# Moving the transposition of V from the DMA queue to TensorE in a layernorm, attention and linear kernel

## The reference

```python
x = x + attn(layernorm(x), Wq, bq, Wk, bk, Wv, bv)
x = x + linear(layernorm(x), weight * scale_weight[:, None], bias)
```

```python
q, k, v = (split_heads(h @ W + b) for W, b in ...)
ctx = local_attention(q, k, v)                  # window of 256 keys
idx = [0] + top_k(norm(q), 62) + [t - 1]
ctx[idx] = softmax(q[idx] @ k.T / 8) @ v
```

## Time and profile before

| | |
|---|---|
| median of 3 runs | 2140.1 us (2135.53 to 2141.93) |
| profiled execution | 2135.53 us |
| its span, first to last instruction | 2134.0 us |
| PE busy | 2102.1 us (99%) |
| PE weight loads busy | 1791.9 us (84%) |
| DVE busy | 1272.7 us (60%) |
| ACT busy | 829.0 us (39%) |
| POOL busy | 502.7 us (24%) |

### The profile page before, as it was taken

The page is one execution under the profiler, slowest core; times in us unless marked ns, Lnnn a source line. Parts: engine busy times, 40 slices in busy tenths (PEclk is TensorE's granted clock), DMA queues, the critical chain, the costliest instruction groups (busy, mean ns, idle before and its releaser), DMA issues.

```text
span 2134.0 us, 36682 instructions
## 1 busy us (share of the span) xinstructions
PE 2102.1 (99%) x12576; PEld 1791.9 (84%) x12576; DVE 1272.7 (60%) x2551; ACT 829.0 (39%) x1979; POOL 502.7 (24%) x336
## 2 busy tenths in 40 slices
PE   6999999999999999999999999999999999999999
PEld 6888888888788888887888888878888888888887
DVE  5685556545855564458555554495555566666664
ACT  4334445552354455532544545225445551000000
POOL 2231122124411321144112211432123112212121
PEclk9999999999999999999999999999999999999999
DMA  4333232223332322233323221323223113333331
GB/s 161 103 99 88 75 106 64 62 69 99 109 90 75 106 60 65 69 95 103 88 85 88 76 68 42 104 69 83 65 71 120 51 59 146 128 138 128 138 128 69
DMA packets 192506, 194.29 MB, mean 91 GB/s; under 512 B 91984, under 2 KB 157590, under 8 KB 192400
## 3 DMA queue, kind: packets, MB, share of 16 engines
q1 hardware_dynamic: 184752, 175.19, 27.7%
q10 hardware_dynamic: 4320, 15.73, 1.8%
q0 software_dynamic: 3328, 2.17, 0.5%
HBM read 122.73 MB, written 51.44 MB: 82 GB/s over the span
## 4 chain that ended last, share of the span: by engine, by line
PE 85%; DVE 11%; issue 2%; ACT 1%; DMA 1%; DVEq 0%; SPq 0%; POOL 0%; ACTq 0%; POOLq 0%
PE proj L566 40%; PE proj L742 15%; PE pv L691 10%; PE turn L679 5%; PE score L664 5%; PE pv L722 3%; DVE top_idx L1317 2%; DVE x_norm L1319 2%; PE score L704 2%; DVE top_val L1315 2%; DVE q_sq L1282 2%; PE turn L714 1%; PE turn L731 1%; PE proj L831 1%; DVE norms L1284 1%
## 5 line engine op out<-in xcount | busy, mean ns | idle before, releaser
L566 PE MATMUL proj<-xT_hi,w_lo 128*128 128x512 f32 x1536 | 408.7, 397 | 0.0
L566 PE MATMUL proj<-xT_hi,w_hi 128*128 128x512 f32 x1536 | 402.8, 404 | 2.5 <-issue 1.5
L566 PE MATMUL proj<-xT_lo,w_hi 128*128 128x512 f32 x1536 | 381.4, 390 | 0.0
L434 POOL CAST w_hi<-w_raw 128x1024 fp32r<-128x1024 f32 x96 | 100.7, 1049 | 1171.6 <-PE proj L566 901.7
L566 PEld LDWEIGHTS proj<-xT_lo,w_hi 128*128 128x128 f32 x1536 | 288.3, 188 | 62.9
L566 PEld LDWEIGHTS proj<-xT_hi,w_lo 128*128 128x128 f32 x1536 | 280.6, 188 | 62.0
L566 PEld LDWEIGHTS proj<-xT_hi,w_hi 128*128 128x128 f32 x1536 | 274.2, 188 | 63.4 <-DVE kT_lo L1300 2.7
L1002 ACT ACTIVATE probs<-score,neg_max 128x256 f32<-128x256 f32 (+1 forms) x512 | 229.3, 463 | 167.4 <-DVE neg_max L1366 120.1
L691 PEld LDWEIGHTS pv<-v_nat,pT 128*128 128x128 f32 x2048 | 248.1, 191 | 10.4
L691 PE MATMUL pv<-v_nat,pT 128*128 128x64 f32 x2048 | 242.3, 271 | 0.0
L436 POOL TENSOR_TENSOR w_lo<-w_raw,w_hi 128x1024 fp32r<-128x1024 f32 x96 | 232.3, 2420 | 7.8
(11 more groups left out here) (165 smaller groups left out, 2988.3 us busy)
## 6 DMA issues: line engine op xcount, KB each, us to landing
w_raw<-in_wstream SPq DMA_DIRECT2D x96, 512.0 KB
x_buf<-in_rows SPq DMA_DIRECT2D x55, 512.0 KB, 4.1
q_rows<-q_nat SPq DMA_DIRECT2D x64, 256.0 KB
ctx_rows<-ctx_out SPq DMA_DIRECT2D x128, 128.0 KB, 1.9
q_store<-ctx_rows SPq DMA_DIRECT2D x30, 512.0 KB
out<-q_store ACTq DMA_DIRECT2D x30, 512.0 KB, 2.6
q_store<-in_cols SPq DMA_DIRECT2D x28, 512.0 KB
q_store<-in_rows SPq DMA_DIRECT2D x8, 512.0 KB, 5.2
```

The lines of the kernel that those rows point to most:

```text
L434: pool.tensor_copy(w_hi[b][:, :], w_raw[b][:, :]).then_inc(w_hi_set, 1)
L566: mm = pe.matmul(proj[:, bank, :], w[b][:, k * P:k * P + P], x[:, k, half * HALF:half * HALF + HALF], start=(m == 0), stop=(m == 23), skip ...
```

## The change

The 16-bit halves, the transposing DMAs and the joining copies go. PE transposes `vT`, which is now packed (1024 columns), against the identity into `misc` in three groups: tiles 0, 8, 1 and 2 after the scores of step 0; tiles 3 to 6 ahead of `turn_p` of step 0; tile 7 ahead of `weigh` of step 0. ACT copies each group to `v_nat` (`v_nat_out`): ahead of the exponentials of step 0, ahead of `p_out` of step 0, and ahead of `p_out` of step 1. The edge tiles have 64 rows; the upper 64 rows of those tiles in `v_nat` are set to zero once. Since `misc` is used in turns, `m_turned` and `m_set` now count four uses a unit. `vT` and `probs` also change places as scratch memory at the start.

```diff
-        vT = sb("vT", [P, (TILES + 1) * P])
-        v_parts, v_turned = (sb(name, [P, TILES + 1, 2, P], U16) for name in ("v_parts", "v_turned"))
+        vT = sb("vT", [P, SEQ])
...
+        V_GROUPS = [[(0, 0), (8, 128), (1, 256), (2, 384)], [(3, 0), (4, 128), (5, 256), (6, 384)], [(7, 0)]]
+        V_PIECES = [[(64, 0, TILES, 2, 0), (P, 1, 1, 2, 256)], [(P, 3, 1, 4, 0)], [(P, 7, 1, 1, 0)]]
...
-            def turn_v(n, hp, h):
-                sp.wait_ge(v_parted, n * (2 * PAIRS) + 2 * hp + h + 2)
-                apart(sp)
-                sp.dma_start_transpose(v_turned[:, V_TILES[h], :, :].rearrange("p t s r -> p (t s) r"),
-                                       v_parts[:, V_TILES[h], :, :].rearrange("p t s c -> p (t s c)")).then_inc(v_moved[h], 16)
...
             def weigh(u, s):
                 pe.wait_ge(pv_free, u * EVENTS + s + 1)
-                if s < 2:
-                    pe.wait_ge(v_set, 2 * u + s + 1)
...
+            def turn_v(u, g, first):
+                if g == 0:
+                    pe.wait_ge(proj_free[0], first + 3)
+                else:
+                    pe.wait_ge(m_set, u * MISC + g)
+                apart(pe)
+                for j, col in V_GROUPS[g]:
+                    a, z = tile_tokens(j)
+                    mm = pe.transpose(misc[0:z - a, col:col + P], vT[:, a:z], ident[:, :])
+                mm.then_inc(m_turned, 1)
...
             def turn_gq(u):
+                pe.wait_ge(m_set, u * MISC + 3)
                 pe.wait_ge(pad_set, u + 1)
...
                 scores(u, 0, first)
+                turn_v(u, 0, first)
                 part(0)
                 if ahead:
                     turn_ahead(1)
+                turn_v(u, 1, first)
                 if ahead:
                     part(1)
...
                 if not ahead:
                     part(1)
+                turn_v(u, 2, first)
                 weigh(u, 0)
...
-            def join_v(u, h):
-                act.wait_ge(v_moved[h], 16 * (u + 1))
-                act.wait_ge(pv_free, u * EVENTS + 1)
-                apart(act)
-                act.copy(v_nat[:, V_TILES[h], :, :].rearrange("p t h d -> p (t h d)").bitcast(U16)
-                                .rearrange("p (t r s) -> p t s r", r=P, s=2), v_turned[:, V_TILES[h], :, :]).then_inc(v_set, 1)
+            def v_nat_out(u, g):
+                act.wait_ge(m_turned, u * MISC + g + 1)
+                for rows, j, step, count, col in V_PIECES[g]:
+                    last = act.copy(v_nat[0:rows, j:j + step * (count - 1) + 1:step, :, :],
+                                    misc[0:rows, col:col + count * P].rearrange("p (t h d) -> p t h d", h=2, d=HD))
+                last.then_inc(m_set, 1)
...
+                v_nat_out(u, 0)
                 exps(u, 0)
-                join_v(u, 0)
                 columns(0)
...
+                v_nat_out(u, 1)
                 p_out(u, 0)
                 exps(u, 1)
-                join_v(u, 1)
                 out(0, 0)
                 columns(1)
+                v_nat_out(u, 2)
                 p_out(u, 1)
...
-            def part_v(n, hp, h):
-                dve.wait_ge(proj_free[0], n * SLICES + PAIRS + 2 * hp + h + 2)
-                apart(dve)
-                tok = slice(V_TILES[h].start * P, V_TILES[h].stop * P)
-                dve.tensor_copy(v_parts[:, V_TILES[h], :, :],
-                                vT[:, tok].bitcast(U16).rearrange("p (t c s) -> p t s c", c=P, s=2)).then_inc(v_parted, 1)
...
-                part_v(n, 0, 0)
                 k_lo_out(n, 0, 0)
...
-                part_v(n, 0, 1)
                 k_lo_out(n, 0, 1)
```

More of the change, by code:

```diff
@@ L20 @@
 U32 = mybir.dt.uint32
-U16 = mybir.dt.uint16
 ALU = mybir.AluOpType
@@ L40 @@
 EVENTS = STEPS + 1
+MISC = 4
 ROUNDS = BATCH + 1
@@ L166, in build @@
         p_turned = sem("p_turned"); pT_set = sem("pT_set")
-        v_parted = sem("v_parted"); v_moved = [sem(f"v_moved{h}") for h in range(2)]; v_set = sem("v_set")
         m_turned = sem("m_turned"); m_hi_set = sem("m_hi_set"); m_set = sem("m_set")
@@ L200, in tile_tokens @@
             return max(0, P * j - 64), min(SEQ, P * j + 64)
-        V_TILES = [slice(0, TILES // 2), slice(TILES // 2, TILES + 1)]
+        V_GROUPS = [[(0, 0), (8, 128), (1, 256), (2, 384)], [(3, 0), (4, 128), (5, 256), (6, 384)], [(7, 0)]]
+        V_PIECES = [[(64, 0, TILES, 2, 0), (P, 1, 1, 2, 256)], [(P, 3, 1, 4, 0)], [(P, 7, 1, 1, 0)]]
         AHEAD_AT = {(5, 0): ("add", 0), (5, 1): ("add", 1), (5, 2): ("moments", 0), (5, 3): ("moments", 1), (5, 4): ("roots", 0),
@@ L340, in stores @@
                 store_ctx(n, hp, 0)
-                if hp < PAIRS - 1:
-                    turn_v(n, hp + 1, 0)
                 if hp == PAIRS - 1 and not following:
@@ L352, in stores @@
                 store_ctx(n, hp, 3)
-                if hp < PAIRS - 1:
-                    turn_v(n, hp + 1, 1)
             def batch(n, following):
@@ L370, in batch @@
                 apart(sp)
-                for h in range(2):
-                    turn_v(n, 0, h)
                 for hp in range(PAIRS):
@@ L699, in global_scores @@
             def global_scores(u):
-                pe.wait_ge(m_set, u + 1)
+                pe.wait_ge(m_set, u * MISC + 4)
                 for qs, ks, first, stop in ((gq_hi, kT_hi, True, False), (gq_lo, kT_hi, False, False),
@@ L906, in _ @@
             act.wait_ge(ident_set, 1)
-            act.copy(pT[:, 0:1], ident[:, 0:1])
+            act.copy(probs[:, 0:1], ident[:, 0:1])
             turn8 = turn[:, :].rearrange("p (k t) -> p k t", k=KC)
@@ L970, in v_out @@
                 apart(act)
-                act.wait_ge(v_parted, n * (2 * PAIRS) + 2 * hp + 1)
-                apart(act)
[L973 to L976, removed]
+                act.activation(vT[:, h * HALF:h * HALF + HALF], proj[:, 0, :], ACT.Identity,
+                               bias=bv_c[:, bass.ds(hp, 1)]).then_inc(proj_free[0], 1)
             def k_hi_out(n, hp, h):
@@ L982, in k_hi_out @@
                                bias=bk_c[:, bass.ds(hp, 1)]).then_inc(k_hi_set[h], 1)
-            def join_v(u, h):
-                act.wait_ge(v_moved[h], 16 * (u + 1))
-                act.wait_ge(pv_free, u * EVENTS + 1)
-                apart(act)
-                act.copy(v_nat[:, V_TILES[h], :, :].rearrange("p t h d -> p (t h d)").bitcast(U16)
-                                .rearrange("p (t r s) -> p t s r", r=P, s=2), v_turned[:, V_TILES[h], :, :]).then_inc(v_set, 1)
+            def v_nat_out(u, g):
[4 more added lines that the diff above has]
+                last.then_inc(m_set, 1)
             def gq_hi_out(u):
-                act.wait_ge(m_turned, u + 1)
+                act.wait_ge(m_turned, u * MISC + MISC)
                 act.copy(gq_hi[:, :], misc[:, 0:P]).then_inc(m_hi_set, 1)
@@ L1098, in batch @@
                 attend(n, PAIRS - 1, following, last=True)
-            spare = [probs[:, :], qT_cur[:, :]]
+            spare = [vT[:, :], qT_cur[:, :]]
             def first_sums(t):
@@ L1164, in _ @@
             dve.memset(zero_c[:, :], 0.0)
-            dve.sem_inc(v_parted, 1)
-            dve.memset(vT[:, HD:P], 0.0)
-            dve.memset(vT[:, SEQ + HD:SEQ + P], 0.0).then_inc(edge_zero, 1)
+            dve.memset(v_nat[HD:P, 0:TILES + 1:TILES, :, :], 0.0).then_inc(edge_zero, 1)
             dve.wait_ge(edge_zero, 1)
@@ L1490, in attend @@
                 pv_out(u, 0)
-                if not last:
-                    part_v(n, hp + 1, 0)
                 maxima(u, 2)
@@ L1530, in attend @@
                 inverses(u, STEPS)
-                if not last:
-                    part_v(n, hp + 1, 1)
                 top_norms(5)
```

## The result

The changed kernel takes 2153.4 us (median of 4 runs, 2150.85 to 2154.79) against 2140.0 for the kernel before (4 runs, 2135.53 to 2141.93): a ratio of 1.0064 with a 95% interval of 1.0046 to 1.0083, 13.4 us slower. The sign was right; the size was not: 24.4 us were forecast, and the range of 2154 to 2184 starts just above the time. The profiled execution took 2151.85 us, with a span of 2150.3 us, 16.3 more than that of the kernel before.

What follows compares the result with a forecast made beforehand. PE at its own pace was taken to bound the kernel, 41.4 us a unit. 33.3 - 6.9 - 2.0 = +24.4 us on the median 2140.1 gave 2164.5 us, range 2154 to 2184.

Steps and rivals of the forecast that it cites:

- no wait of PE for the new copies: ACT's copies out of misc in each unit: 1.0 us of slack, so waits costed at nothing.
- the last unit: Last unit's projections and turn_p: 0.46 + 1.3 + 0.3 = 2.0 us of waits gained back.
- What is added to PE: Nine transposes in each of 32 units, priced at 1.04 us a unit as in line 714's stream: 33.3 us.
- the upper bound: Added transposes at 0.121 each plus a 0.17 us gap per group: 1.60 us a unit, 51 us.
- The lower bound: Added transposes at 0.099 each, from line 714's eight: 0.89 us a unit, 28.4 us in all.
- The widening: Range for the whole kernel widened from 2159 to 2182 to 2154 to 2184, as runs differ by some 0.3%.
- The heads: Heads of batches: waits for kT_lo and the exponentials go without part_v, 1.6 and 5.3 us, 6.9 gained.
- The comparison of medians: Whole kernel: +24.4 us moved from the profiled 2135.5 to the median 2140.1, giving 2164.5.
- the second (recorded duration): Rival: 288 transposes cost their recorded 0.272 us each, 78 us less 9, giving 2209; chance 0.04.
- the third: Rival: transposes cost PE nothing measurable, fitting in 5.6 us a unit that look open: 2131 to 2140; chance 0.04.
- the fourth: Rival: faster, as DMA traffic holds up PE's operand reads in every unit; with 1.5 us back, 2116; chance 0.03.
- The first: Rival: ACT detour through misc does not fit, 0.5 to 1 us lost a unit, 2180 to 2197; chance 0.07.

Runs made afterwards that it cites:

- experiments 1: Kernel before with part_v, the transposing DMAs and join_v left out, v_nat set to zero: 2126.3 us, ratio 0.9954.
- experiment 2: Kernel before with nine transposes a unit added at the places of the change, results unread: 2162.8 us, ratio 1.0128.
- Experiment 4: Changed kernel with every transpose of v done twice into the same place: 2184.5 us, ratio 1.0225.
- experiment 5: Changed kernel with part_v's copies back on DVE at their old places, into an unread buffer: 2158.3 us, ratio 1.0108.
- 6: Kernel before with part_v of each batch's first unit moved on DVE behind what PE waits for: 2129.7 us, ratio 0.9969.
- Experiment 3: Changed kernel with its first group of four transposes moved behind the first projection after the scores: 2155.5 us, ratio 1.0090.
- 9: Kernel before with only POOL's add_bias of the linear stage's second tile waiting until DVE has normalised the third: 2134.7 us, ratio 0.9981.
- experiment 10: Changed kernel run again without alteration, beside further runs of the kernel before: 2152.4 us, ratio 1.0063.
- the first set: First of three sets of experiment runs; the kernel before, run beside it, had a median of 2136.67 us.
- the lower bunch: Seven of the 15 unchanged runs of the kernel before beside the last set: 2136.0 to 2137.5 us, median 2137.1.

## Why the prediction was wrong

What held: PE's pace sets the time; what was saved on DVE, ACT and the DMA queues was worth nothing in the middle units (experiments 1, 2); no wait of PE for the new copies, even with the transposes doubled (4); the price by pitch and not by record, 273 to 286 ns long and 0.096 apart on average; the head waits were for the most part `part_v`'s (5, 6); the last unit gave back 1.9 us for a forecast of 2.0 (2.06 by its terms).

**The step that failed is the term "What is added to PE"**: 32 x 1.04 = 33.3 us, measured 32 x 0.865 = 27.7. The mechanism was right and the size was off by 5.6 us. I took the nine transposes of `turn_gp`, one block between projections, and gave their price to three groups. At that price the groups are 0.46, 0.46 and 0.12 us; they are 0.32, 0.43 and 0.12. So nearly all of it is the first group, behind the scores. Experiment 3 shows that the place is part of it: behind a projection the same four cost 0.41. The way from the scores back to a projection costs something already in the kernel before, and four transposes in between take some of it over. The 0.05 from 0.41 to 0.46 no run explains, and why the way from the scores costs what it costs none shows. I had looked at these neighbours and found only that they might cost more, a gap of 0.17 us for each group in the upper bound; that one might be saved did not come up. Experiment 4 gives the other side: where the place is paid for, the second nine cost 1.01. The lower bound, 0.099 each or 28.4 us, was itself above the 27.7 measured, so the range as worked out, from 2159 on, had no room for this term. The widening to 2154 had: with 27.7 and the other terms as forecast the time is 2140.1 + 27.7 - 6.9 - 2.0 = 2158.9. It took the differences below as well to fall under 2154.

**The heads**: 6.9 us forecast, 8.1 read from the stages, 1.2 more. The scaled idle times were a little short. The 8.1 have two parts. 3.5 us are the price of the four units' own transposes, which the old waits would have covered anyway (experiment 2), and 4.6 are what the heads got shorter beyond that (521.7 against 517.1). That is why experiment 5 returns 5.3 us at the heads and not 8.1.

**The linear stage**: nothing forecast, 2.5 us in this pair of profiles, 1.7 of them by where POOL's addition fell (9, 10), 0.8 behind the issue of the last store, cause open. The opening took 1.0 us longer in the same pair. Together, with 0.1 for the last unit: 24.4 - 5.6 - 1.2 + 0.1 - 2.5 + 1.0 = 16.2, against 16.3 us in the spans.

**The comparison of medians**: 13.4 us where the profiles have 16.3. The median of three of the kernel before, 2140.1, lies near the runs with a clock of 0.998 (the clocks of the runs behind it are not on record); the profiled execution had 1.00, and so had all of the changed kernel. Against the nine runs of the kernel before at 0.999 to 1.000 beside the first set, with a median of 2136.7, the change costs 2153.4 - 2136.7 = 16.7 us, near the 16.3 of the spans, though these runs were not taken side by side; beside its own set it was 15.3 (experiment 10). I had moved the sum from the execution to the median of the runs shown, which supposes that both kernels' medians lie equally far above; the changed kernel's lay 1.6 above its profiled execution and not 4.6. These 3.0 us and the 8.1 between 24.4 and 16.3 are the whole way from 2164.5 to 2153.4. The mis-sized term and the comparison alone would have left it at 2164.5 - 5.6 - 3.0 = 2155.9, inside the range; the heads and the linear stage brought it below 2154. That it fell just outside and not just inside was in part the luck of the executions.

The rivals: the second (recorded duration) is out by 50 us; the third and the fourth are out, as a unit grew by 0.865 us and did not shrink without the old path. The first did not happen.

## What to carry to other kernels

Where one engine runs without a gap, price an added instruction by the difference between two starts around the very place where it will stand, and look at the kind of work on both sides: here four transposes cost 0.32 us beside a change of work that was paid already, and 0.41 in a stream. Before moving work from an idle engine to the one that sets the time, look whether its order on the idle engine is what costs; here two calls moved on DVE gave 6 us, and with one move on ACT and one wait on POOL it was 10.8 against the lower bunch (2137.1 - 2126.3), where the change lost 15 to 17. Before a few microseconds are explained by stages, compare the mean clock of the runs: here runs 4 us apart differed by 0.001 to 0.002 in it.

## What the runs showed of the hardware

A VectorE tensor_scalar over 128x1024 took 0.80 to 1.07 us without a GpSimd tensor_tensor of 128x1024 beside it and 3.24 to 3.64 with one, while that one took 2.39 to 2.41 us, as it does alone. In the kernel before the VectorE instruction had started 0.57 us earlier and ended 0.56 us after the other (1789.87 + 3.53 = 1793.40 against 1790.44 + 2.40 = 1792.84): 0.57 + 2.40 + 0.56 = 3.53, as if it stood still meanwhile. PE waited 1.5 us for it, and one wait on GpSimd removed it. The Trainium skill (SBUF — State Buffer, SBUF: two separate sides) says that such a pair does not share its port but that one blocks the other. With that the trace agrees. The same page of the Trainium skill also says that the one that starts first keeps the port for its whole instruction; by the start times of these records it was the later one that did. The granted clock was 1.00, the 2.4 GHz level, in every profiled execution, that with 18 added transposes a unit included, and between 0.998 and 1.000 as the mean of whole runs; the runs at 0.998 were some 4 us longer.
